# Splitting a recurrence's input products into bfloat16 parts, and moving two of its neighbours, in a fused four-layer kernel

## The reference

```python
x = x + ffn0(cond0(x, cond))
x = x + bitlinear_ffn(first_recurrence(cond, x, W, b, alpha))
x = x + moe_ffn(second_recurrence(cond, x, W_z, U_z, C_z, b_z, W_r, U_r, C_r, b_r, W, U, C, b))
x = x + ffn3(moe3(x, cond))

def step(h, xs):                      # the second recurrence
    z = sigmoid(xz + h @ U_z + vz)
    r = sigmoid(xr + h @ U_r + vr)
    hh = tanh(xh + r * h @ U + vh)    # xz, xr, xh = seq @ W_z, seq @ W_r, seq @ W
    h_new = (1.0 - z) * h + z * hh
    return h_new, h_new
```

## Time and profile before

| | us |
|---|---|
| median of 3 runs | 2891.3 (2890.06 to 2892.74) |
| the profiled execution's own time | 2897.34 |
| its span in the trace | 2896.0 |
| PE busy | 2670.2 (92% of the span) |
| DVE busy | 2053.8 (71%) |
| ACT busy | 1610.6 (56%) |
| mean granted TensorE clock | 0.623 |

### The profile page before, as it was taken

How to read it: one execution, slowest core, us unless ns; L and a number is a source line. 1 busy time by engine, 2 the same in 40 slices (tenths; PEclk the granted TensorE clock), 3 DMA queues, 4 the chain that set the end, 5 groups by cost and what they waited for, 6 DMA issues and landing times.

```text
span 2896.0 us, 149960 instructions
## 1 busy us (share of the span) xinstructions
PE 2670.2 (92%) x59796; PEld 2275.6 (79%) x59796; DVE 2053.8 (71%) x12169; ACT 1610.6 (56%) x8445; POOL 340.7 (12%) x457
## 2 busy tenths in 40 slices
PE   7689999999999999999999999999769999969995
PEld 4468989989899898998989989888747777744332
DVE  5688888877777777777777777665457776666228
ACT  3445555566666666666666666554335565621115
POOL 0000101011010010100101001010124444410000
PEclk7555555555555555555555555555569999979997
DMA  4132323212221232212312122200459766342000
GB/s 136 33 113 84 105 81 90 76 42 89 64 89 57 75 95 64 84 57 80 95 59 84 59 78 92 61 19 5 158 189 316 243 208 203 87 165 73 0 0 30
DMA packets 171227, 270.90 MB, mean 94 GB/s; under 512 B 23418, under 2 KB 127757, under 8 KB 168229
## 3 DMA queue, kind: packets, MB, share of 16 engines
q1 hardware_dynamic: 122852, 196.52, 21.7%
q10 hardware_dynamic: 32368, 31.12, 3.8%
q0 software_dynamic: 15312, 33.67, 3.4%
HBM read 170.77 MB, written 98.70 MB: 93 GB/s over the span
## 4 chain that ended last, share of the span: by engine, by line
PE 82%; DVE 8%; ACT 3%; issue 3%; SPq 2%; DMA 1%; ACTq 0%; POOL 0%; POOLq 0%; DVEq 0%
PE work L678 9%; PE bank_h L688 7%; PE bank_g L688 7%; PE bank_r L688 7%; PE bank_z L688 7%; PE work L688 5%; PE bank_h L697 4%; PE bank_g L697 4%; PE bank_r L697 3%; PE bank_z L697 3%; PE work L915 3%; PE bank_z L915 3%; PE work L938 2%; PE bank_h L938 2%; PE work L1024 2%
## 5 line engine op out<-in xcount | busy, mean ns | idle before, releaser
L688 PEld LDWEIGHTS work<-h_run,hi_r 128*128 128x128 f16 x4092 | 227.2, 112 | 171.6 <-DVE h_run L1801 158.9
L1801 DVE TENSOR_TENSOR_SCAN h_run<-z_run,hh_run 128x12 f16<-128x12 f32 x1024 | 186.8, 182 | 232.2 <-ACT hh_run L1224 213.0
L688 PE MATMUL work<-h_run,hi_r 128*128 128x2 f16 x4092 | 284.9, 173 | 65.7 <-DVE h_run L1801 61.3
L1224 ACT ACTIVATE hh_run<-bank_h 128x4 f32<-128x4 f32 x1024 | 180.2, 176 | 276.9 <-PE bank_h L697 276.8
L1205 ACT ACTIVATE r_guess<-work 128x4 f32<-128x4 f32 x1023 | 177.5, 173 | 237.2 <-PE work L688 220.0
L1786 DVE TENSOR_TENSOR_SCAN rh_run<-r_run,h_run 128x12 f16<-128x12 f32 x1023 | 187.1, 183 | 151.1 <-ACT r_run L1214 66.2
L688 PE MATMUL bank_g<-h_hi,hi_g 128*128 128x2 f16 x4092 | 253.2, 166 | 39.0 <-ACT h_hi L1194 38.5
L1219 ACT ACTIVATE z_run<-bank_z 128x4 f32<-128x4 f32 x1024 | 180.3, 176 | 149.8 <-PE bank_z L697 4.8
L697 PE MATMUL bank_h<-rh_run,hi_h 128*128 128x2 f16 x4092 | 258.1, 167 | 1.2 <-DVE rh_run L1786 0.6
L688 PE MATMUL bank_h<-h_run,hi_h 128*128 128x2 f16 x4092 | 253.6, 166 | 3.5 <-DVE h_run L1783 3.3
L697 PE MATMUL bank_g<-h_lo,hi_g 128*128 128x2 f16 x4092 | 253.1, 166 | 2.0 <-issue 0.6
(11 more groups left out here) (481 smaller groups left out, 8086.1 us busy)
## 6 DMA issues: line engine op xcount, KB each, us to landing
stage<-in_gate_up SPq DMA_DIRECT2D x128, 384.0 KB
stage<-in_down SPq DMA_DIRECT2D x128, 192.0 KB
gu_split<-parts SPq DMA_DIRECT2D x64, 384.0 KB
gu_ring<-gu_split SPq DMA_DIRECT2D x64, 384.0 KB, 3.8
xt<-x_rows ACTq DMA_DIRECT2D x191, 128.5 KB, 3.3
x_rows<-zero_rows SPq DMA_DIRECT2D x64, 257.0 KB, 3.2
yk<-y_rows SPq DMA_DIRECT2D x16, 1024.0 KB, 4.8
dn_split<-parts SPq DMA_DIRECT2D x64, 192.0 KB
```

The lines of the kernel that those rows point to most:

```text
L688: ins = pe.matmul(o[:, m, step, :], w[:, k, m * P:(m + 1) * P], hi(k), start=False, stop=False, skip_group_check=True)
L1224: act.activation(two(t.hh_run[:, :, 1]), gate_in(t.h, c2, s2), ACT.Tanh, scale=scale_of["h"]).then_inc(s.hh_act, 1)
L1801: dve.tensor_tensor_scan(t.h2_run[:, 0:3 * KH * B], threes(t.z_run), threes(t.hh_run), 0.0, ALU.mult, ALU.add).then_inc(s.h2hi, 1)
```

## The change

It makes the float32 input products out of bfloat16 ones. The weights and x are each cut into three bfloat16 parts whose sum is the value; the first part is the upper half of the float32 word, read in place with a step of two elements (`first8`), the others are made by DVE with subtractions. Six of the nine products of parts are kept. A product of one output half m is then 6 x 2 = 12 bfloat16 matmuls of 128x128 weights by 64 columns, and all 12 stand in one `beside`, so a gate and half takes two ticks. The products of chunk 0 for g1, made before the ticks, stay float32.

Input products now stand at places 26 to 31, 44 to 49 and 58 to 61; the fills at B 28, 29, 30 and A 31, B 46, 47, 48 and A 49, and A 59 and 61. LAG is 96, so that the second recurrence's chunk begins at place 32. x is split in DVE's places (B 25 and A 25 for the current chunk, B 55 and B 56 for the one two chunks on), the weights in 16 operations on 128x512 elements in ticks 18 to 41. Of ffn1's end, ACT's scaling moves from place 22 to 23, and both turns of o1 stand at place 24.

```diff
--- before.py
+++ after.py
@@ -56,7 +56,7 @@
 PRODUCTS = ((0, 0), (0, 1), (1, 0))
 
 HALF = STEPS // 2
-LAG = STEPS + 37
+LAG = STEPS + 32
 TICKS = T + LAG
 ROWS, PACE = 10, 2
 FRONT = ROWS + PACE * TOPK
@@ -64,6 +64,7 @@
 
 halves = lambda a: a.rearrange("(k p) n -> p k n", p=P)
 flat = lambda a: a.rearrange("p k n -> p (k n)")
+first8 = lambda a: a.bitcast(BF16)[:, :, 1::2]
 two = lambda a: a.rearrange("p (k b) -> p k b", k=KH)
 pairs = lambda a: a.rearrange("p c two -> p (c two)")
 threes = lambda a: a.rearrange("p c three -> p (c three)")
@@ -120,7 +121,7 @@
     x_turned xT gu_mm silu mid mid_turned midT yt
     tl0 tl1 tl2 tl3 tl4 tl5 tl6 tl7 tl8 tl9 tl10 tl11
     yo0 yo1 yo2 yo3 yo4 yo5 yo6 yo7 yo8 yo9 yo10 yo11
-    max3 peak3 wq3 wts_in wts_exp yk0 yk1 yk2 acc acc_mm x2
+    in_split max3 peak3 wq3 wts_in wts_exp yk0 yk1 yk2 acc acc_mm x2
     tb_mm tb router_mm scores comb_sb comb_mm combT sh_mm sg s_in
     he_mm he_act he o2_mm y3 ext ar inv rounded xq f1 h3_mm h3 hq o3_mm xo stores
     dve
@@ -151,19 +152,43 @@
 def inputs_at(tau):
 
     c, i = place_at(tau)
-    if 0 <= c < NCH and 25 <= i < 37:
-        return ("r", "z", "h")[(i - 25) // 4], c, 0, (i - 25) % 4
-    if 0 <= c < NCH and 44 <= i < 56:
-        return ("r", "z", "h")[(i - 44) // 4], c, 1, (i - 44) % 4
-    if 56 <= i < 64 and c + 2 < NCH:
-        return "g1", c + 2, (i - 56) // 4, (i - 56) % 4
+    for half, first in ((0, 26), (1, 44)):
+        if 0 <= c < NCH and first <= i < first + 6:
+            return ("r", "z", "h")[(i - first) // 2], c, half, (i - first) % 2
+    if 58 <= i < 62 and c + 2 < NCH:
+        return "g1", c + 2, (i - 58) // 2, (i - 58) % 2
     return None
 
 
+
+
+SPLIT_X = {(25, "B"): ("x1", 0), (25, "A"): ("x1", 1), (55, "B"): ("x0", 0), (56, "B"): ("x0", 1)}
+
+
+def split_x_at(tau, place):
+
+    c, i = place_at(tau)
+    what, step = SPLIT_X.get((i, place), (None, None))
+    if what == "x1" and 0 <= c < NCH:
+        return what, c, step
+    if what == "x0" and c + 2 < NCH:
+        return what, c + 2, step
+    return None
+
+
+
+IN_SPLIT = {("g1", 1): 2}
+for _c in range(NCH):
+    IN_SPLIT["x1", _c] = len(IN_SPLIT) + 2
+    if _c + 2 < NCH:
+        IN_SPLIT["g1", _c + 2] = len(IN_SPLIT) + 2
+
+IN_PRODUCTS = ((0, 0), (0, 1), (0, 2), (1, 0), (1, 1), (2, 0))
+
 FILL_B, FILL_A = {}, {}
-for _half, _first in ((0, 29), (1, 48)):
-    FILL_B.update({_first: ("guess", _half), _first + 1: ("r", _half), _first + 4: ("z", _half)})
-    FILL_A.update({_first + 7: ("h", _half), 59 + 4 * _half: ("g1", _half)})
+for _half, _first in ((0, 28), (1, 46)):
+    FILL_B.update({_first: ("guess", _half), _first + 1: ("r", _half), _first + 2: ("z", _half)})
+    FILL_A.update({_first + 3: ("h", _half), 59 + 2 * _half: ("g1", _half)})
 
 
 def fill_at(tau, place):
@@ -216,18 +241,23 @@
 VIDEO_BIAS = (30, 31, 32)
 W_SUMS, W_MEAN, W_SCALE = 25, 37, 42
 
+SPLIT_INPUTS_A = {20: ("rest", "g1"), 21: ("rest", "z"), 23: ("rest", "r"), 38: ("rest", "h"), 39: ("third", "z"),
+                  40: ("third", "r"), 41: ("third", "h")}
+SPLIT_INPUTS_B = {18: ("first", "g1"), 19: ("first", "z"), 20: ("first", "r"), 21: ("first", "h"), 24: ("third", "g1"),
+                  25: ("second", "g1"), 26: ("second", "z"), 27: ("second", "r"), 39: ("second", "h")}
+
 W_QUANT = range(43, 55)
 PREPARE = 55
 FIRST_PIECES = 58
 FFN1_A = (1, 2, 3, 7, 9, 11, 13, 14, 15, 16, 17, 24)
 FFN1_B = (2, 3, 7, 8, 9, 10, 11, 12, 13, 14, 15, 16, 17)
-FFN1_E, FRONT_E = (4, 6, 8, 10, 12, 18, 19, 20, 21, 22), (0, 4, 5)
+FFN1_E, FRONT_E = (4, 6, 8, 10, 12, 18, 19, 20, 21, 23), (0, 4, 5)
 FRONT_A, FRONT_B = (2, 3, 4, 5, 6, 7, 8), (3, 4, 5, 6, 7, 8, 9, 10)
 
 
 def is_free(tau, place):
     f, e = ffn1_at(tau), front_at(tau)
-    return not (f and f[1] in (FFN1_A if place == "A" else FFN1_B) or fill_at(tau, place)
+    return not (f and f[1] in (FFN1_A if place == "A" else FFN1_B) or fill_at(tau, place) or split_x_at(tau, place)
                 or e and e[1] in (FRONT_A if place == "A" else FRONT_B) or pads_at(tau))
 
 
@@ -297,6 +327,9 @@
         sb = in_scope(recurrent)
         t.rec = {g: sb("rec_" + g, [P, KH, D]) for g in GATES}
         t.inp = {g: sb("inp_" + g, [P, KH, D]) for g in GATES}
+
+        t.inp3 = {g: sb("inp3_" + g, [P, 3, KH, D], BF16) for g in GATES}
+        t.x_rest, t.x_low = sb("x_rest", [P, KH, P]), sb("x_low", [P, KH, P], BF16)
         t.vid = {g: sb("vid_" + g, [P, KH, D]) for g in GATES[1:]}
         t.bcol = sb("bcol", [P, len(GATES), KH])
         t.bias = {g: sb("bias_" + g, [P, KH, B]) for g in GATES}
@@ -668,16 +701,28 @@
             if q == 1:
                 ins.then_inc(s.p0, 1)
 
-    def input_products(g, c, half, n):
-
-        m, k = divmod(n, KH)
+    def first_input_products(half):
+
+        for m in range(KH):
+            at = half * HALF * B
+            out = input_bank(t, "g1", 0, half)[:, m * P + at:m * P + at + HALF * B]
+            for k in range(KH):
+                ins = pe.matmul(out, t.inp["g1"][:, k, m * P:(m + 1) * P], t.xf[:, k, at:at + HALF * B],
+                                start=(k == 0), stop=(k == KH - 1))
+        ins.then_inc(s.in_mm, 1)
+
+    def input_products(g, c, half, m):
+
         at = half * HALF * B
         out = input_bank(t, g, c, half)[:, m * P + at:m * P + at + HALF * B]
-        if n == 0 and FILLS[g, c, half] > 2:
+        x = (first8(t.xf[:, :, chunk_cols(c)]), first8(t.x_rest), t.x_low)
+        if m == 0:
             pe.wait_ge(s.fill, FILLS[g, c, half] - 2)
-        ins = pe.matmul(out, t.inp[g][:, k, m * P:(m + 1) * P], t.xf[:, k, chunk_cols(c)][:, at:at + HALF * B],
-                        start=(k == 0), stop=(k == KH - 1))
-        if n == 3:
+        for a, b in IN_PRODUCTS:
+            for k in range(KH):
+                ins = pe.matmul(out, t.inp3[g][:, a, k, m * P:(m + 1) * P], x[b][:, k, at:at + HALF * B],
+                                start=((a, b, k) == (0, 0, 0)), stop=((a, b, k) == (2, 0, KH - 1)))
+        if m == KH - 1:
             ins.then_inc(s.in_mm, 1)
 
     def big_products(bank, w, c, step, hi):
@@ -757,13 +802,11 @@
                 ins = pe.matmul(w0[:, 0:D], t.q2T[:, j, :], t.wq["down"][:, j, :], start=(j == 0), stop=(j == NI - 1))
             if i == 22:
                 ins.then_inc(s.f_pe, 1)
-        elif i in (23, 24):
-            k = i - 23
-            if k == 0:
-                pe.wait_ge(s.f_act, FA * c + A_O1)
-            ins = pe.transpose(w1[:, k * P:(k + 1) * P], t.o1[:, k * P:(k + 1) * P], t.ident)
-            if k == 1:
-                ins.then_inc(s.f_pe, 1)
+        elif i == 24:
+            pe.wait_ge(s.f_act, FA * c + A_O1)
+            for k in range(KH):
+                ins = pe.transpose(w1[:, k * P:(k + 1) * P], t.o1[:, k * P:(k + 1) * P], t.ident)
+            ins.then_inc(s.f_pe, 1)
 
     def front(c, j):
         w0, w1 = work[0], work[1]
@@ -800,14 +843,14 @@
         elif tau in OPEN_BANKS:
             open_bank(t.bank_of[OPEN_BANKS[tau]])
         elif inputs_at(tau):
-            g, c, half, n = inputs_at(tau)
-            if (g, half, n) == ("r", 0, 0):
-                pe.wait_ge(s.x1, c + 1)
-            if (g, half, n) == ("z", 1, 0) and c >= 1:
+            g, c, half, m = inputs_at(tau)
+            if (g, half, m) == ("r", 0, 0):
+                pe.wait_ge(s.in_split, IN_SPLIT["x1", c])
+            if (g, half, m) == ("z", 1, 0) and c >= 1:
                 pe.wait_ge(s.fr_dve, RD * (c - 1) + R_LOW)
-            if g == "g1" and n == 0:
-                pe.wait_ge(s.d0, len(D0))
-            input_products(g, c, half, n)
+            if (g, half, m) == ("g1", 0, 0):
+                pe.wait_ge(s.in_split, IN_SPLIT["g1", c])
+            input_products(g, c, half, m)
         elif ffn1_at(tau):
             ffn1(*ffn1_at(tau))
         elif pads_at(tau):
@@ -824,8 +867,7 @@
     open_bank(t.g1)
     pe.wait_ge(s.d0, D0["x0", 0, KH - 1])
     for half in range(2):
-        for n in range(4):
-            input_products("g1", 0, half, n)
+        first_input_products(half)
     for tau in range(END):
         t1, t2 = steps_at(tau)
         if t1 is not None:
@@ -1126,7 +1168,7 @@
             act.wait_ge(s.f_pe, FP * c + (P_T01, P_T23)[n // 2])
             act.copy(flat(t.q2T)[:, slice_cols(n)],
                      (w1, w2)[n // 2].bitcast(BF16)[:, slice_cols(n % 2)]).then_inc(s.f_act, 1)
-        elif i == 22:
+        elif i == 23:
             act.wait_ge(s.f_dve, FD * c + D_DOWN)
             act.wait_ge(s.f_pe, FP * c + P_DN)
             act.activation(t.o1, w0[:, 0:D], ACT.Copy, scale=t.tok["down"]).then_inc(s.f_act, 1)
@@ -1498,6 +1540,34 @@
         w, j = divmod(n, KH * INNER // BLK)
         return flat(t.w1_f32[("gate", "up", "down")[w]])[:, blk_cols(j)], w, j
 
+    def split_x(what, c, step):
+        xc = t.xf[:, :, chunk_cols(c)]
+        if step == 0:
+            if what == "x1":
+                dve.wait_ge(s.x1, c + 1)
+            else:
```

(30 more changed lines are left out.)

## The result

The changed kernel took 2901.2 us (median of 7 runs, 2900.3 to 2906.6), the one before 2892.7 on the same chip (7 runs, 2890.1 to 2894.7). The medians differ by 8.4 us, where 8.8 were forecast. The ratio of the two, which is worked out from all runs and is not the quotient of the medians (1.0029), is 1.0036. Its 95% interval is 1.0026 to 1.0046, or 7.5 to 13.3 us: the kernel is slower, and the forecast lies inside.

What follows compares the result with a forecast made beforehand. Bound: each tick's loop through PE, ACT and DVE, with 0.41 us of cover for other PE work. Terms -33.6, +50.6, +0.2, -6.4, -4.5, +1.0, 0 and +1.5 sum to +8.8 on 2891.3: 2900.1 us, range 2889 to 2912.

Steps and rivals of the forecast that it cites:

- -33.6: Middle stage: 460 float32 input products, one a tick, each showing 0.073 us, are taken away, saving 33.6 us.
- +50.6: Middle stage: 230 ticks of 768 columns each exceed the cover by 0.22 us, adding 50.6 us (43.7 to 57.5).
- first two rivals: 64-column matmuls hold PE's array for less (net 2886, chance 0.08) or for longer (2975 or 3022, chance 0.07).
- third rival: PE's clock rises to 2.4 GHz in the denser ticks, so 768 columns are wholly covered: 2850 us, chance 0.05.
- -6.4: LAG 101 to 96: five ticks fewer of the first stage at 1.28 us each, saving 6.4 us.
- the splits' +1.5: Ticks 18 to 41: seven weight splits in place A add 0.12 us each, nine in B about 0.07; 1.5 us together.
- -4.5: Place 22: moving ACT's scaling to place 23 removes its wait for PE's down product, 14 x 0.32 us saved.
- fifth rival: The mend does nothing, as ACT's scaling delays the next tick at place 23 too: +4.5, 2905 us, chance 0.05.
- I count 0: Place 24: DVE's sum, starting some 0.2 us later behind both turns, costs nothing, at worst 1.4 us.
- fourth rival: DVE becomes late through the x splits, its sum at place 24 and the weight splits: +7 more, 2907, chance 0.09.
- Splitting x, 0: 31 pairs of DVE operations on 256 columns fit their places at no cost; +3.1 us if the cover is gone.
- Routing moves with LAG, 0: Routing and its DMA issues on POOL and SP move five ticks earlier against ffn1 and add nothing.

## Why the prediction was right

The sum was +8.8 and the ticks gave +8.0, the medians +8.4. Its main terms held one by one. Four smaller misses nearly cancel, and that the sum came within 1 us is luck: the ticks of two executions of the kernel before are 2.2 us apart.

- **Input products.** -33.6 held: the ticks that lost one are at 1.827. The +50.6 came out as 230 x 0.207 = 47.6, at 0.01 us a tick less and within its bounds. Net +14.0 instead of +17.0. The cover of 512 columns, read off the four turns and the down product, is exact to the resolution of the three widths run: 512, 640 and 768 columns cost 0, 0.10, 0.207. The first two rivals fall: a 64-column matmul holds the array as long as its columns, and reading x with a step costs nothing. The Trainium skill (TensorE: Matmul & The Clock Gate, Back-to-back issue gap) says that in a stream of pairs the weight load has its share in the spacing, and gives figures for 128 and 512 columns. With 64 columns, for which it gives none, no such share is seen here: twelve pairs in 0.61 us are the columns alone.
- **Clock.** 0.50 through the middle stage, as before. The third rival falls.
- **Last stage.** 96 ticks from 1951.1 to 2126.3 us, 1.825 each, where 101 took 1.830: the 12 groups fit there, +0.2 or less.
- **LAG.** The first stage went from 140.2 to 135.2 us, -5.0, where -6.4 and the splits' +1.5 make -4.9. Its own ticks give -6.4 for the five, +0.7 for the splits, -0.4 and +0.8 for ticks 19 and 58, whose reason is open (tick 58 alone differs by 0.3 between two executions of the kernel before); 0.3 is left.
- **The mend.** -4.5 held, 14 x 0.326 by the medians of the place. ACT's scaling now starts with no idle time behind g_pairs, and the next gate is not late, so the fifth rival falls:

```profile
...
1021.51 0.17 ACT L1269 ACTIVATE g_pairs<-bank_g 128x4 f32<-128x4 f32 x1
1021.58 0.47 ACT L1174 ACTIVATE o<-work,tok_down 128x256 f32<-128x256 f32 x1
1022.05 0.17 ACT L1247 ACTIVATE r_guess<-work 128x4 f32<-128x4 f32 x1
```

- **DVE's sum at 24, not 0.** The place costs +0.10 and not 0.073, 1.4 us instead of 1.0. Place 24, its turns, DVE's sum behind them, and the x split in the next place B:

```profile
...
1023.16 0.67 PE L808 MATMUL work<-ident,o 128*128 128x128 f32 x2
...
1023.62 0.29 PE L733 MATMUL work<-h_run,hi_r 128*128 128x2 f16 x4
...
1023.86 0.42 DVE L1668 TENSOR_TENSOR x<-x,work 128x256 f32<-128x256 f32 x1
...
1024.20 0.17 DVE L1861 SCALAR_TENSOR_TENSOR h_run<-r_guess,h 128x4 f16<-128x4 f32 x1
...
1024.31 0.24 PE L742 MATMUL bank_z<-h_run,hi_z 128*128 128x2 f16 x4
...
1024.42 0.27 PE L733 MATMUL bank_h<-h_run,hi_h 128*128 128x2 f16 x4
...
1024.55 0.24 PE L733 MATMUL bank_h<-h_run,lo_h 128*128 128x2 f16 x4
...
1024.78 0.42 DVE L1550 TENSOR_TENSOR x_rest<-x 128x256 f32<-128x256 f32 x1
...
1025.05 0.18 ACT L1266 ACTIVATE hh_run<-bank_h 128x4 f32<-128x4 f32 x1 [0.28 <-PE bank_h L742]
1025.26 0.18 DVE L1879 TENSOR_TENSOR_SCAN h_run<-z_run,hh_run 128x12 f16<-128x12 f32 x1
```

  The next tick starts 0.46 after the turns, as behind an input product, which is 0.05 more than in a plain tick. PE's second group of four, for bank_r, starts 0.15 behind the first (1023.77), where a plain tick has 0.13 (1117.74 and 1117.87 in the plain stretch). These two make the 0.07 of a float32 product, as forecast. The other 0.03 come from DVE. Its sum holds the product of r_guess and h until 1024.20, so that this ends at 1024.37. PE's first group that reads it starts at 1024.42, and the next one 0.13 behind it instead of 0.11; together the two are 0.03 late. So "I count 0" was wrong by 14 x 0.03 = 0.4 us, which is also what came true of the fourth rival (at most 7 us).
- **Splitting x, 0.** In the last rows the split ends at 1025.20, ACT's tanh at 1025.23, and the scan starts at 1025.26: hidden, as forecast.
- **Splitting the weights, mis-sized.** +1.5 forecast, +0.7 measured. The seven in place A cost 0.13 in four ticks and 0.05 to 0.07 in three, near the 0.12 each; the nine in place B cost nothing where 0.07 each was counted.
- **Row issues, missed.** The term that the prediction did not have: POOL's row issues stand at fixed places of the second recurrence, odd ones from 47 to 61 before and even ones from 42 to 56 after. Before, float32 input products stood in all eight of those ticks (in the last chunk in five), and they last 1.90 with a row issue or without. After, five of the eight are plain and three (44, 46, 48) hold bfloat16 products, and by the medians of the places each is 0.014 to 0.027 us longer: 8 plain ticks with four issues take 14.70 us, 8 x 1.827 = 14.62, so 0.02 for each. Over the chunks, long ticks aside, that sums to 1.6 us. "Routing moves with LAG, 0" is the step that failed. The plain ticks pay only in the chunks in which DVE also has a slice of the splitting of the expert weights there, as in this one, whose scan is at 706.09:

```profile
...
706.50 0.47 DVE L1793 SCALAR_TENSOR_TENSOR parts<-stage,moe_up,parts 96x256 f16<-96x256 f32 x1
...
706.90 0.15 DVE L1861 SCALAR_TENSOR_TENSOR h_run<-r_guess,h 128x4 f16<-128x4 f32 x1
...
707.11 0.27 PE L733 MATMUL bank_h<-h_run,hi_h 128*128 128x2 f16 x4
...
```

  DVE's slice starts 0.41 us behind the scan, in the next tick, which has no row issue, 0.38, and the product of r_guess and h is later by as much. PE's groups for bank_h, which read it, are 0.02 to 0.03 late, as at place 24. Without the slice, in plain ticks of chunks 2 and 14, a row issue costs nothing (1.828). What the three ticks with bfloat16 products pay for is not shown. In the kernel before DVE's slice is late in the same way (0.41), but behind a float32 product PE reads 0.07 later and does not wait. An operation that is moved takes along what it costs; that cost had been lying under another one.

By stage, then: the middle one was forecast at 17.0 - 4.5 + 1.0 and five ticks of the last one's length, 9.1, in sum 22.6. It gave 22.6, as 14.0 - 4.5 + 1.4 + 1.6 + 9.1 = 21.6 and 1.0 that falls to single long ticks; two executions of the kernel before differ there by 1.4.

The prediction's reason for the sign stands too: PE's work shrank by 62 us and the time grew, because of 768 columns only 512 had cover. Laid out to that cover, over half as many ticks again, the same splits gain 0.67%.

## What to carry to other kernels

Where a loop's engine stands idle for a fixed answer time in each round, that gap is the unit in which side work is free: lay the work out in pieces of that size, over more rounds, rather than in fewer and larger pieces, and count the overhang times the rounds, not the busy time. Moving other things of the schedule (here a lag) exposes what they cost where their old cover was. Once all gaps are full, the count of instructions can become the price: here a third fewer matmuls with the same number of columns were 11 us faster.
